# Query products behind the sums of all four row tiles of x, and the query weight behind x in one queue

## The reference

```python
def cond(v, q, W3, b3, W2, b2):                  # v = x (32, 64, 512), q (32, 256)
    q_emb = relu(q @ W3 + b3)                    # (32, 512)
    v_sum = sum(v, axis=1, keepdims=True)
    x = (n * v + v_sum) * q_emb[:, None, :]      # n = 64
    return relu(x @ W2 + b2)

def ffn(x, W_fc, W_proj):                        # (2048, 512), (512, 2048)
    w1, w2 = ternary(W_fc), ternary(W_proj)      # groups of 64: round(w / mean|w|) clipped to -1..1, times mean|w|
    h = square(relu(x @ w1.T))                   # (32, 64, 2048)
    return rms_norm(h) @ w2.T

out = x + ffn(cond(x, q, W3, b3, W2, b2), W_fc, W_proj)
```

## Time and profile before

| What | Value |
|---|---|
| Median of 3 runs | 311.33 us (311.01 to 311.59) |
| The profiled execution | 311.10 us |
| Its span, first to last instruction | 309.3 us |
| Mean granted TensorE clock | 1.000 |
| PE busy | 304.5 us, 98% |
| ACT, DVE, POOL busy | 191.2, 187.2, 115.0 us |
| DMA | 27.03 MB, 87 GB/s on average |

### The profile page before, as it was taken

One profiled execution on the slowest core, in us unless ns is written; L12 is line 12 of the kernel. 1 busy time (PEld: TensorE's weight loads), 2 busy tenths in 40 slices (PEclk: granted clock), 3 DMA queues, 4 the chain that ended last, 5 costly groups with the idle time before them and its releaser, 6 DMA issues.

```text
span 309.3 us, 3792 instructions
## 1 busy us (share of the span) xinstructions
PE 304.5 (98%) x1279; PEld 232.6 (75%) x1279; DVE 187.2 (61%) x311; ACT 191.2 (62%) x282; POOL 115.0 (37%) x106
## 2 busy tenths in 40 slices
PE   8999999999999999999999999999999999999995
PEld 8654545447888888888888888888888888888883
DVE  0689999994888778886257335942223484222245
ACT  1773566796999599976746444455554445555540
POOL 1044676646433323335333331353333314333330
PEclk9999999999999999999999999999999999999999
DMA  7993743362654044113005200340000034000003
GB/s 259 366 312 120 223 117 105 102 139 65 196 147 102 1 102 37 34 34 68 2 0 170 103 0 1 136 139 0 0 0 2 0 136 138 0 0 0 2 2 137
DMA packets 30293, 27.03 MB, mean 87 GB/s; under 512 B 17689, under 2 KB 19777, under 8 KB 30273
## 3 DMA queue, kind: packets, MB, share of 16 engines
q1 hardware_dynamic: 29936, 26.22, 29.3%
q10 hardware_dynamic: 336, 0.56, 0.5%
HBM read 18.39 MB, written 4.19 MB: 73 GB/s over the span
## 4 chain that ended last, share of the span: by engine, by line
PE 98%; DVE 0%; issue 0%; DVEq 0%
PE ps_out L382 38%; PE ps_acc L370 38%; PE ps_acc L354 18%; PE ps_out L341 2%; PE ps_out L332 1%; PE ps_acc L425 1%; PE ps_x L442 1%; PE ps_x L416 0%; DVE x_sb L587 0%; DVE x_t L517 0%; PE ps_x L422 0%; PE ps_acc L429 0%; PE ps_acc L437 0%; DVEq L504 0%
## 5 line engine op out<-in xcount | busy, mean ns | idle before, releaser
L265 POOL TENSOR_TENSOR wv_sb<-wv_sb 128x512 f32<-128x512 f32 x55 | 71.8, 1306 | 122.6 <-DVE y_lo L532 115.5
L370 PE MATMUL ps_acc<-h_hi,w_t 128*128 128x512 f32 x256 | 100.0, 391 | 0.0
L382 PE MATMUL ps_out<-w_t,y_hi 128*128 128x512 f32 x256 | 100.0, 391 | 0.0
L382 PE MATMUL ps_out<-w_t,y_lo 128*128 128x512 f32 x256 | 99.7, 389 | 0.0
L370 PE MATMUL ps_acc<-h_lo,w_t 128*128 128x512 f32 x256 | 99.6, 389 | 0.0
L530 DVE CAST y_hi<-x_t 128x512 fp32r<-128x512 f32 x64 | 32.6, 510 | 87.5 <-PE ps_out L382 73.0
L679 ACT ACTIVATE x_t<-ps_acc 128x512 f32<-128x512 f32 x64 | 37.9, 592 | 62.5 <-PE ps_acc L370 62.5
L354 PE MATMUL ps_acc<-x_t,wv_sb 128*128 128x512 f32 x128 | 56.3, 593 | 0.3 <-DVE x_t L517 0.3
L370 PEld LDWEIGHTS ps_acc<-h_lo,w_t 128*128 128x128 f32 x256 | 48.1, 188 | 10.2 <-issue 0.2
L370 PEld LDWEIGHTS ps_acc<-h_hi,w_t 128*128 128x128 f32 x256 | 48.0, 188 | 10.2 <-issue 0.2
L382 PEld LDWEIGHTS ps_out<-w_t,y_lo 128*128 128x128 f32 x256 | 48.1, 188 | 9.9
(11 more groups left out here) (60 smaller groups left out, 172.7 us busy)
## 6 DMA issues: line engine op xcount, KB each, us to landing
x_sb<-in_x_dram SPq DMA_DIRECT2D x5, 1024.0 KB, 5.4
raw<-in_L_ffn_W_fc_dram SPq DMA_DIRECT2D x8, 512.0 KB, 6.3
raw<-in_L_ffn_W_proj_dram SPq DMA_DIRECT2D x8, 512.0 KB, 4.2
out_dram<-x_sb SPq DMA_DIRECT2D x16, 256.0 KB, 2.1
x_odd<-in_x_dram SPq DMA_DIRECT2D x2, 1024.0 KB, 7.8
x_sb<-in_x_dram SPq DMA_DIRECT2D x4, 256.0 KB, 4.2
wv_sb<-in_L_cond_W_dram SPq DMA_DIRECT2D x4, 256.0 KB, 7.6
x_t<-in_L_cond_W_dram ACTq DMA_DIRECT2D x1, 512.0 KB, 4.7
```

What stands on the lines that cost most here:

```text
L265: engine.tensor_tensor(acc, acc, y_sq[:, v % SQ_RING, :], ALU.add).then_inc(sq_added, 1)
L370: last = pe.matmul(ps_acc[:, (UNITS + v) % ACC_RING, :], w_t[:, j, k * P:(k + 1) * P], part[:, k, g * BANK:(g + 1) * BANK], start=(k == 0 ...
L382: last = pe.matmul(ps_out[:, t, :], part[:, v % RING, t * P:(t + 1) * P], w, start=(opens(v) and part is y_hi), stop=(closes(v) and part i ...
```

## The change

- `WARM_UP` is 6 instead of 7.
- The two transposes of `cond`, and that of the biases, stand behind the sums of tile 2; all three are behind one semaphore (`condt_done`), and `biases_turned` is gone.
- The query products stand behind the sums of tile 3, ahead of the first unit of h0.
- The load of `wq_sb` goes from ACT's queue, where it was second, to SP's queue, behind the four tiles of x and ahead of `load_wv(0)`.

```diff
-WARM_UP = 7
+WARM_UP = 6
...
             for t in range(TT):
                 sp.dma_start(x_sb[:, t, :], x_rows[0, :, t, :]).then_inc(x0_loaded[t], 16)
+            sp.dma_start(wq_sb[:], w_q.rearrange("(k p) d -> p k d", p=P)).then_inc(wq_loaded, 16)
             load_wv(0)
...
             for i in range(WARM_UP):
                 pe.matmul(ps_acc[:, 1, 0:P], zeros, zeros, start=True, stop=True)
-            pe.wait_ge(ident_ready, 1)
-            pe.wait_ge(cond_loaded, 16)
-            for k in range(KQ):
-                last = pe.transpose(ps_acc[:, 0, k * BATCHES:(k + 1) * BATCHES], cond_sb[:, k * P:(k + 1) * P],
-                                    ident_f[0:BATCHES, 0:BATCHES])
-            last.then_inc(condt_done, 1)
             pe.wait_ge(consts_ready, 1)
             for t in range(TT):
-                if t == TT // 2:
-                    pe.wait_ge(condt_ready, 1)
-                    pe.wait_ge(biases_loaded, 32)
-                    pe.transpose(ps_acc[:, 0, KQ * BATCHES:KQ * BATCHES + 2 * KD], bias_sb,
-                                 ident_f[0:2 * KD, 0:2 * KD]).then_inc(biases_turned, 1)
-                    pe.wait_ge(wq_loaded, 16)
-                    for m in range(KD):
-                        for k in range(KQ):
-                            last = pe.matmul(ps_x[:, m * BATCHES:(m + 1) * BATCHES], wq_sb[:, k, m * P:(m + 1) * P],
-                                             cond_t[:, k, :], start=(k == 0), stop=(k == KQ - 1))
-                    last.then_inc(q_done, 1)
                 pe.wait_ge(x0_loaded[t], 16)
                 for k in range(KD):
                     last = sum_x_block(0, t, k)
                     if t == TT - 1:
                         last.then_inc(xt_done, 1)
+                if t == TT - 2:
+                    pe.wait_ge(ident_ready, 1)
+                    pe.wait_ge(cond_loaded, 16)
+                    for k in range(KQ):
+                        pe.transpose(ps_acc[:, 0, k * BATCHES:(k + 1) * BATCHES], cond_sb[:, k * P:(k + 1) * P],
+                                     ident_f[0:BATCHES, 0:BATCHES])
+                    pe.wait_ge(biases_loaded, 32)
+                    pe.transpose(ps_acc[:, 0, KQ * BATCHES:KQ * BATCHES + 2 * KD], bias_sb,
+                                 ident_f[0:2 * KD, 0:2 * KD]).then_inc(condt_done, 1)
+            pe.wait_ge(condt_ready, 1)
+            pe.wait_ge(wq_loaded, 16)
+            for m in range(KD):
+                for k in range(KQ):
+                    last = pe.matmul(ps_x[:, m * BATCHES:(m + 1) * BATCHES], wq_sb[:, k, m * P:(m + 1) * P],
+                                     cond_t[:, k, :], start=(k == 0), stop=(k == KQ - 1))
+            last.then_inc(q_done, 1)
...
             dve.wait_ge(condt_done, 1)
             dve.tensor_copy(cond_t, ps_acc[:, 0, 0:KQ * BATCHES].rearrange("p (k b) -> p k b", k=KQ)).then_inc(condt_ready, 1)
-            dve.wait_ge(biases_turned, 1)
...
             act.dma_start(cond_sb, cond).then_inc(cond_loaded, 16)
-            act.dma_start(wq_sb[:], w_q.rearrange("(k p) d -> p k d", p=P)).then_inc(wq_loaded, 16)
             act.dma_start(bias_sb[0:KD, :], b_q.rearrange("(m p) -> m p", p=P)).then_inc(biases_loaded, 16)
```

More of the change, by code:

```diff
@@ L188, in adaln_ffn @@
         biases_loaded = sem("biases_loaded")
-        biases_turned = sem("biases_turned")
         biases_ready = sem("biases_ready")
```

## The result

The changed kernel takes 313.40 us (median of 6 runs, 312.57 to 313.80) against 311.17 us (6 runs, 310.69 to 311.59): a ratio of 1.0074, 95% interval 1.0063 to 1.0085. That is 2.23 us slower by the medians, where 0.72 was forecast, and outside the stated range. The direction and the place were forecast; one term of about 1.7 us was missing from the sum.

The account below looks back on a forecast made before the run. PE was taken as the bound, busy 304.5 of 309.3 us. The head's terms put the first unit at 12.05 against 11.31: 311.33 + 0.74 = 312.07, stated as 312.05; range 311.4 to 312.65, forecast's own 311.75 to 312.35.

Parts of the forecast that it names:

- the sum: Whole kernel: first unit of h0 0.74 us later, passed to the end one to one, giving 312.05 us.
- part 1: Head of PE's queue: first sum starts at 3.72 instead of 4.38, worth a gain of 0.35 us.
- The rise: PE's clock at the head: goes from 1.2 to 2.4 GHz at about 5.8 us; each microsecond later costs 0.48 us.
- The two clock rivals: First clock rise comes earlier (10%; 311.05 us if at 3.7) or later (5%; 313.0 us if two microseconds later).
- a first unit after 12.4: Sign that the forecast is wrong: h0's first unit starting after 12.4 us, where about 12.0 was expected.
- part 2: Transposes of cond and biases behind tile 2's sums: cost +0.16 us, bounds 0.12 and 0.26.
- part 3: Query products last, ahead of h0: 1.28 us of hand-overs come into the open; first unit at 12.05 against 11.31.
- part 4: Query weight moved to SP's queue: tile 3 lands near 6.2, weight near 7.6; gives nothing and costs nothing.
- The late-weight rival: Query weight lands at 9.05 behind x, with tile 3 still near 7.6: 312.35, up to 312.6 us (12%).
- part 5: Behind the first unit: ACT reaches its weights 1.6 us later, but slack covers it; cost nothing.

Follow-up runs that it names:

- e4: Kernel before with only six warm-up products and the two transposes of cond behind tile 0; ratio 0.9993 to before.
- e1: Changed kernel with five products of zeros, 128 columns wide, filling PE's wait ahead of the first unit of h0; ratio 1.0027 to before.
- e8: Changed kernel with query products of 128 columns instead of 32, the wait behind them left empty; ratio 1.0018 to before.
- e3: Kernel before with two idle DVE instructions ahead of the first x1_t, so PE waits 1.4 us; ratio 1.0047 to before.
- e7: Changed kernel with five products of zeros, 32 columns wide, in PE's wait ahead of the first unit; ratio 1.0036 to before.
- e9: Changed kernel with query blocks 0 and 1 in PSUM banks of their own, each signalled, so ACT and DVE start early; ratio 0.9998 to before.
- e11: Kernel before with four idle DVE instructions ahead of the first x1_t, so PE waits 2.6 us; ratio 1.0113 to before.
- e6: Changed kernel with the seventh warm-up product put back; ratio 1.0075 to before.
- e12: Changed kernel with the query weight's load back on ACT's queue; ratio 1.0079 to before.
- e10: Kernel before with only the query weight's load moved to SP's queue behind x; ratio 1.0071 to before.
- e14: Changed kernel with two products of zeros, 128 columns wide, in PE's wait, filling 0.45 us of it; ratio 1.0072 to before.

## Why the prediction was wrong, by its own steps

**The start of the first sum** (part 1) was put at 3.72, at most 3.80. It is 3.81: the warm-up ends at 3.68 by the chain, tile 0 is there by then, and PE took 0.13 us from there. The eight other kernels with six products have 3.61 to 3.88.

**The rise** was 6.7 instead of 5.8 in this execution. At the 0.48 us for each microsecond that part 1 worked out, that is 0.44 us of the first unit's 1.15. Over the fourteen profiles the rise lies between 3.6 and 6.8, with no order by what the head of PE's queue does (5.2 with six products in e4, 6.7 with six in the changed kernel). So I take it for scatter between executions and not for a cost of the change. The Trainium skill, TensorE: Matmul & The Clock Gate, section What's actually happening, says that the moment of the rise is not tied to the kernel's start and differs from run to run; the fourteen profiles, in all of which PE begins at 0.78, agree. The two clock rivals were about this moment and did not decide. The prediction's sign "a first unit after 12.4" came true by 0.06 us, and only through this rise.

**The transposes** (part 2): from the end of tile 2's passes to tile 3's, 0.25 + 0.16 = 0.41 us were forecast. The last pass of tile 2 starts at 7.85 and the first of tile 3 at 8.34: less one distance of 0.11, that is 0.38.

**The query products last** (part 3): from the end of the last to the first unit, 1.28 us were forecast; the chain has 11.21 to 12.46, 1.25. With the rise taken back to 5.8, the first unit would start at 12.02; the forecast was 12.05 (its own terms, 10.79 and 1.28, give 12.07). e1 and e8, which lack the fall, are 0.84 and 0.56 us above before, on both sides of the 0.74 of the sum.

**The query weight** (part 4): the loads of the changed kernel by line, with us to landing:

```profile
L297 SPq DMA_DIRECT2D x_sb<-in_x_dram x4: 391/416/479, 0.7 to 2.1; - x4
...
DMA to landing us min/median/max: 2.9/3.3/4.2
```

```profile
L298 SPq DMA_DIRECT2D x_t<-in_L_cond_W_dram x1: 434/434/434, 2.6 to 2.6; - x1
...
DMA to landing us min/median/max: 6.1/6.1/6.1
```

The last tile landed at 6.3 (6.2 forecast), the weight at 8.7 (7.6 forecast). The late-weight rival had 9.05, nearer than my own figure, though its reason, that tile 3 still lands near 7.6, did not come true. Between 4.5 and 5.5 us the DMA engines moved 229 GB/s here against 369 before, 0.14 MB less, which is some 0.4 of the 1.1 us that the weight is late; the rest is open. In the eight other kernels with this queue it landed at 7.8 to 8.3. It cost nothing here, since PE came to it at 9.3 and not at 8.8; with the rise at 5.8 it would have been 8.9, only just behind the landing.

**What is behind** (part 5): no further wait of PE, as forecast.

**The step that failed is the sum**: "+0.74 us on the first unit, which goes to the end one to one". It priced the wait of 1.3 us by its length, and took each pass after it at the upper level: a fall of the clock behind the wait was put at nothing, without a reason. The rows before did not show a fall, and I asked only when the clock rises, never whether 1.4 us without work, directly behind 1.8 us of 32-column passes, could bring it down again. That missing term is 1.70 us in the trace; by the ratios it is 1.5 (changed less e1) to 1.7 (changed less e8). With it the sum is 0.74 + 1.70 = 2.44 against 2.23 measured.

Of the cause, this is shown: in the changed kernel it takes the wait and the narrow passes ahead of it together to make the clock fall in every run. Wide products in the wait take the fall away (e1: none in ten), and so do wide query products with the wait as it was (e8: none in ten; e3, a wait behind wide sums: none in six). Neither of the two is needed in every case: e7 and e9 have falls with no wait for the first unit in their profiled runs (three and one in ten), and e11 behind wide sums with a longer one (two in four). Putting the seventh product back, or the old queue, does not take it away (e6, e12). Not shown is how the chip comes to the verdict. e7, e9, e10 and e11 have falls in some runs and not in others, from the same instructions, so the moment of the execution plays a part too. The Trainium skill, TensorE: Matmul & The Clock Gate, section HAM oscillation — how this bites in real kernels, tells of falls behind waits for transfers, all of them longer than these. The trace does not agree that only such waits matter: 1.3 us behind narrow passes were enough in all six runs.

## What to carry to other kernels

When a change puts a chain of small engines (here ACT, DVE, PE: 1.25 us) in the open, price the wait twice: its length, and half of the time that PE then works at the lower clock if the clock falls. In this kernel narrow products next to the wait made the fall likelier, so keep them among wide ones, make them wide where that costs no time (e8), or leave their consumer something to start on early (e9). Look at the granted clock of each run, not of the profiled one alone: a mean of 0.995 in a kernel whose neighbour has 1.000 is a whole stretch at the lower level. Then look where it lies: behind PE's last pass it costs nothing.

## What the runs showed of the hardware that was not expected

- The clock fell for 3.4 us at a time, 1.70 us of lost work in the changed kernel, behind a wait of only 0.73 us in e14; by the mean clock it also fell in three runs of e7 with the wait filled, each time with 32-column passes near; and not behind 1.3 and 1.4 us with 128-column passes ahead (e8, e3).
- In the four profiles that have it, the fall began 6.8 us behind the first rise and lasted 3.4 us, wherever the wait stood.
- Ten passes of zeros, which compute nothing, made a kernel 1.5 us faster (e1).
- The moment of the first rise moved over 3.2 us between executions (3.6 to 6.8 us), at 0.48 us of time for each: by an estimate 1.5 us in all, enough for the 1 us by which the runs of the kernel before scatter, though no run here ties the two.
